# Rows of the feed-forward blocks transposed by DMAs instead of by TensorE, in a cross attention and mixture-of-experts kernel

## The reference

```python
def attention(Q, K, V, causal):
    scores = einsum('bqd,bkd->bqk', Q, K) / sqrt(d_k)          # causal: masked
    return einsum('bqk,bkd->bqd', softmax(scores), V)
def xattn(y, Z):                                               # no projections
    y = layernorm(y + attention(y, y, y, causal=True), g1, beta1)
    y = layernorm(y + attention(y, Z, Z, causal=False), g2, beta2)
    ff = relu(y @ w1 + b1) @ w2 + b2                           # 256 -> 1024 -> 256
    return layernorm(y + ff, g3, beta3)
def moe(h):                                                    # 8 experts, each row uses 2
    topk_w, topk_idx = top_k(softmax(h @ wg.T), 2)             # weights normed to 1
    return sum over the two of weight * ((silu(h @ w1[e].T) * (h @ w3[e].T)) @ w2[e].T)
x = x + xattn(layernorm(x), ctx)
x = x + moe(layernorm(x))
```

## Time and profile before

| | us |
|---|---|
| median of 3 runs | 558.45 (558.25 to 559.0) |
| the profiled execution, own time | 560.24 |
| its span, first to last instruction | 557.8 |
| TensorE busy in the span | 503.5 (90%) |
| VectorE, ScalarE, GpSimd busy | 383.5, 291.2, 294.7 |
| mean granted clock of TensorE | 0.982 of full |

### The profile page before, as it was taken

One profiled execution on the slowest core, in us unless ns is written; L12 is line 12 of the kernel. 1 busy time (PEld: TensorE's weight loads), 2 busy tenths in 40 slices (PEclk: granted clock), 3 DMA queues, 4 the chain that ended last, 5 costly groups with the idle time before them and its releaser, 6 DMA issues. The chain is left out here.

```text
span 557.8 us, 11154 instructions
## 1 busy us (share of the span) xinstructions
PE 503.5 (90%) x3753; PEld 333.2 (60%) x3753; DVE 383.5 (69%) x977; ACT 291.2 (52%) x592; POOL 294.7 (53%) x331
## 2 busy tenths in 40 slices
PE   4999999979899998899999977779999899999981
PEld 2676766745566675577565666545566556666651
DVE  5799886688877577867876789988767534344440
ACT  2647867574747546673558373564554333443420
POOL 3564030016423519826795629473667565667564
PEclk9999999999999999999999999999999999999995
DMA  8021615238878257832765543125795688787763
GB/s 273 2 71 25 198 58 152 77 71 160 155 170 141 86 73 145 175 90 77 147 142 135 162 101 125 39 76 105 122 182 97 114 113 124 131 127 132 132 86 38
DMA packets 131090, 64.57 MB, mean 116 GB/s; under 512 B 105533, under 2 KB 122366, under 8 KB 131038
## 3 DMA queue, kind: packets, MB, share of 16 engines
q1 hardware_dynamic: 123550, 53.64, 44.2%
q0 software_dynamic: 7488, 10.23, 11.5%
HBM read 28.19 MB, written 10.35 MB: 69 GB/s over the span
## 5 line engine op out<-in xcount | busy, mean ns | idle before, releaser
L1132 PE MATMUL ps<-arena,probT 128*128 128x256 f16 (+2 forms) x1092 | 181.8, 320 | 7.0 <-DMA probT<-prob 4.4
L1132 PEld LDWEIGHTS ps<-arena,probT 128*128 128x128 f16 (+1 forms) x1092 | 105.8, 98 | 65.5 <-issue 10.3
L901 POOL DMA_INDIRECT out<-y,qst x39 | 62.5, 1604 | 28.3 <-issue 13.9
L946 ACT ACTIVATE prob<-ps,nbias 128x512 f16<-128x512 f32 x64 | 39.0, 610 | 71.5 <-DVE nbias L1647 71.5
L1132 PE MATMUL ps<-arena,qT 128*128 128x512 f16 (+1 forms) x384 | 70.8, 337 | 5.4 <-DVE prob L1782 5.3
L2181 DVE SCALAR_TENSOR_TENSOR ps<-ps,w1m 128x512 f32<-128x512 f32 x39 | 27.4, 703 | 54.6 <-ACT w1m L1075 54.5
L1075 ACT ACTIVATE w1m<-ps 128x512 f32<-128x512 f32 x39 | 23.3, 597 | 75.5 <-PE ps L1132 75.5
L1132 PE MATMUL ps<-arena,tT 128*128 x468 | 58.2, 276 | 2.8 <-DVE tT L2277 2.8
L1132 PEld LDWEIGHTS ps<-arena,qT 128*128 128x128 f16 x384 | 33.0, 98 | 41.2 <-issue 8.4
L1132 PE MATMUL ps<-tT 128*128 128x512 f16 (+3 forms) x240 | 52.7, 360 | 2.1 <-DVE tT L1609 2.1
L1132 PE MATMUL ps<-w2s,tT 128*128 128x256 f16 x384 | 48.4, 273 | 5.7 <-DVE tT L1850 5.6
(11 more groups left out here) (216 smaller groups left out, 983.0 us busy)
## 6 DMA issues: line engine op xcount, KB each, us to landing
stage<-we_in SPq DMA_DIRECT2D x33, 256.0 KB, 2.9
prob<-we_in SPq DMA_DIRECT2D x15, 256.0 KB, 2.9
xin<-x_in SPq DMA_DIRECT2D x16, 128.0 KB, 2.8
out<-y SPq DMA_DIRECT2D x16, 128.0 KB
hrow<-tT SPq DMA_DIRECT2D x4, 512.0 KB, 3.1
y<-x_in SPq DMA_DIRECT2D x3, 512.0 KB, 6.4
stage<-z_in SPq DMA_DIRECT2D x4, 256.0 KB, 5.2
prob<-w_in SPq DMA_DIRECT2D x4, 256.0 KB, 2.9
```

Of the source, the lines that this page charges most:

```text
L901: g.indirect_dma_start(out[:rows_of(p), :], bass.IndirectOffsetOnAxis(ridx[:, n:n + 1], 0), ys[:, n % RING, :], None, compute_op=ALU.add). ...
L946: a.activation(row_cols(q, 0, c), ps[c][:, :w], ACT.Exp, bias=nbias[:, q, :], scale=SM)
L1132: r = t.matmul(o, lhs(a), rhs(b), start=first and n == 0, stop=last and n == 2)
```

## The change

For tiles 0 to 13 the rows of `y` no longer go through TensorE. Tile by tile, ScalarE copies the row tile to 16 bits (`y_row_hi`), VectorE subtracts (`y_row_lo`), and SP issues two DMA transposes of 128x256 (`y_turn`). The halves lie in `nrm`, the buffer of the layer norm on GpSimd, for tiles 0 to 11 (so `ln_affine` waits for the transposes two tiles back), and in the query row's place for tiles 12 and 13. Only unit 4 keeps the transposes on TensorE. Three orders change too: SP issues a step's three transposes of exponentials ahead of the step's weight loads, not one ahead and two behind; VectorE's norm of the last self-attention block stands behind the low halves of step 1, not ahead of them; in the last expert tile VectorE's copy of the transposed rows stands ahead of the scaling of the tile before. In units 1 and 2 ScalarE's copy of `h` moves behind the first relu. Left out below: new semaphores, a shorter `psY`, and calls of `y_trans` and `y_lo` that go or lose an argument.

```diff
--- before.py
+++ after.py
@@ -209,6 +209,19 @@
             return stage[:, t % 2, CH:PW].bitcast(F16)[:, :2 * D]
+        def y_row(n):
+            return nrm[:, n % 2, :].bitcast(F16) if n < 3 * TB else q_row(n)
+        def y_turned(n, a):
+            m = n % TB
+            if n < 3 * TB:
+                home = prow if a else ph.rearrange("p (q c) -> p q c", q=2)
+                return home[:, :, ROW + m * P:ROW + (m + 1) * P]
+            at = a * 2 * NT * P + ROW
+            return ph[:, at:at + KD * 2 * P].rearrange("p (k c) -> p k c", k=KD)[:, :, m * P:(m + 1) * P]
@@ -606,6 +619,17 @@
+            def y_turn(n):
+                wait(sp, "y_rlo", n + 1)
+                if n >= TB:
+                    wait(sp, "f_up", KF * (n // TB))
+                else:
+                    wait(sp, "s_pv", NT)
+                for a in range(2):
+                    sp.dma_start_transpose(y_turned(n, a), y_row(n)[:, a * D:(a + 1) * D]
+                                           ).then_inc(sm[f"y_t{n % 2}"], 16)
             def loads(n0, n1):
@@ -616,12 +640,13 @@
             for i in range(NT - 1):
+                if i - 1 in FIRST and i < NT - 2:
+                    y_turn(i - 2)
                 if i + 3 < NT:
                     q_turn(i + 3)
-                turn(i + 1, 0)
+                for p in range(len(TURNS)):
+                    turn(i + 1, p)
                 loads(step_from(i), step_from(i) + STEP_PIECES[i])
-                turn(i + 1, 1)
-                turn(i + 1, 2)
                 if i == 0:
@@ -632,6 +657,8 @@
                     if u == 2:
+                        y_turn(NT - 4)
+                        y_turn(NT - 3)
                         for m in range(6):
@@ -639,6 +666,8 @@
                     load_x(n)
+                if 0 < i < NT - 3 and i not in FIRST:
+                    y_turn(i - 1)
@@ -735,6 +764,8 @@
                 pool.wait_ge(sm[pre + "rstd"], i + 1)
+                if 2 <= i < 3 * TB + 2:
+                    pool.wait_ge(sm[f"y_t{q}"], 32 * (i // 2))
                 g.tensor_scalar(nrm[:, q, :], u[:, q, :], mv[:, q, 0:1], rstd[:, q, :], ALU.subtract,
@@ -780,7 +811,9 @@
-                wait(pool, "f_ytr", j + 1 if j < 3 else len(UNITS))
+                wait(pool, "y_rlo", min(TB * (j + 1), NT - 2))
+                if j == NB - 1:
+                    wait(pool, "f_ytr", 1)
                 for m in range(TB):
@@ -988,16 +1021,22 @@
                     c_exps(i + 1, c)
-                    if i == NT - 2 and c == 0:
-                        y_hi(3)
                 if i + 4 < NT:
                     q_hi(i + 4)
                 split_step(split_hi, act_, i + 1)
-            def y_hi(u):
-                wait(act_, "f_ytr", u + 1)
+                if 0 < i < NT - 2:
+                    y_row_hi(i - 1)
+            def y_row_hi(n):
+                wait(act_, "c_y", n + 1)
+                if n >= 3 * TB:
+                    wait(act_, f"c_q{n % 2}", 16 * ((n - 1) // 2 + 1))
+                copy(y_row(n)[:, :D], y[:, n, :]).then_inc(sm["y_rhi"], 1)
+            def y_hi():
+                wait(act_, "f_ytr", 1)
                 for k in range(KD):
-                    copy(ybT(u, 0, k)[:, cols(u)], psY(u, k)).then_inc(sm["f_yhi"], 1)
+                    copy(ybT(4, 0, k)[:, cols(4)], psY(k)).then_inc(sm["f_yhi"], 1)
@@ -1032,6 +1071,12 @@
                     relu(u, f)
+                    if u in (1, 2) and f == 0:
+                        h_hi(u - 1)
+                    if u < 3 and f == 4:
+                        y_row_hi(TB * (u + 1))
+                    if u == 2 and f == 5:
+                        y_row_hi(NT - 3)
                     if u in (1, 2) and f in (3, 4):
@@ -1050,18 +1095,14 @@
                 else:
-                    c_exps(i + 1, 0)
-                    y_hi(u)
-                    for c in range(1, C_CH):
+                    for c in range(C_CH):
                         c_exps(i + 1, c)
                     if i + 4 < NT:
                         q_hi(i + 4)
-                    if u:
-                        h_hi(u - 1)
                 ffn(u)
                 if not last:
                     split_step(split_hi, act_, i + 1)
-            y_hi(4)
+            y_hi()
             ffn(4)
@@ -1259,25 +1300,23 @@
-            def y_trans(u, i):
-                j, m0, n = UNITS[u]
-                pe.wait_ge(sm["c_y"], TB * j + m0 + n)
-                if u == 0:
-                    pe.wait_ge(sm["c_qlo"], 3)
-                elif u < 4:
-                    wait(pe, "n_u", TB * u)
-                else:
-                    pe.wait_ge(sm["c_u"], NT)
+            def y_trans():
+                j, m0, n = UNITS[4]
+                wait(pe, "c_y", NT)
+                wait(pe, "c_u", NT)
                 for k in range(KD):
                     for m in range(n):
-                        r = t.transpose(psY(u, k)[:, m * P:(m + 1) * P], y[:, TB * j + m0 + m, k * P:(k + 1) * P],
+                        r = t.transpose(psY(k)[:, m * P:(m + 1) * P], y[:, TB * j + m0 + m, k * P:(k + 1) * P],
                                         ident[:])
                 r.then_inc(sm["f_ytr"], 1)
             def up(u, f):
                 n, w = u * KF + f, UNITS[u][2] * P
-                if f == 0:
-                    wait(pe, "f_ylo", KD * (u + 1))
+                if f == 0 and u < 4:
+                    for q in range(2):
+                        wait(pe, f"y_t{q}", 32 * ((UNITS[u][0] * TB + UNITS[u][2]) // 2))
+                elif f == 0:
+                    wait(pe, "f_ylo", KD)
                 if u < 4 and f < 3:
@@ -1294,7 +1333,8 @@
                 if f == 0:
-                    wait(pe, "f_ylo", KD * (u + 1))
+                    if u == 4:
+                        wait(pe, "f_ylo", KD)
                     if u != 3:
@@ -1806,8 +1843,6 @@
                 q = i % 2
-                if i == 0:
-                    s_norm(NB - 1)
                 split_step(split_lo, dve, i)
@@ -1823,9 +1858,9 @@
                 early[0]()
-                if i == NT - 2:
-                    y_lo(3)
                 between(early[1:], own)
+                if i == 0:
+                    s_norm(NB - 1)
                 sums("c_", 1 - q, C_CH, i + 1, C_CH * (i + 2))
@@ -1833,15 +1868,21 @@
                     x1_aggr(FIRST[i - 3])
+                if 0 < i < NT - 2:
+                    y_row_lo(i - 1)
                 for f in late:
                     f()
                 if late:
                     c_bias(i + 2, q)
-            def y_lo(un):
+            def y_row_lo(n):
+                wait(dve, "y_rhi", n + 1)
+                v.tensor_tensor(y_row(n)[:, D:], y[:, n, :], y_row(n)[:, :D], ALU.subtract).then_inc(sm["y_rlo"], 1)
+            def y_lo():
                 for k in range(KD):
-                    wait(dve, "f_yhi", KD * un + k + 1)
-                    v.tensor_tensor(ybT(un, 1, k)[:, cols(un)], psY(un, k), ybT(un, 0, k)[:, cols(un)],
+                    wait(dve, "f_yhi", k + 1)
+                    v.tensor_tensor(ybT(4, 1, k)[:, cols(4)], psY(k), ybT(4, 0, k)[:, cols(4)],
                                     ALU.subtract).then_inc(sm["f_ylo"], 1)
@@ -2081,9 +2122,7 @@
                 split_step(split_lo, dve, i)
-                c_los(i + 1, 0)
-                y_lo(un)
-                for c in range(1, C_CH):
+                for c in range(C_CH):
                     c_los(i + 1, c)
@@ -2100,6 +2139,10 @@
                     split_chunk(split_lo, dve, un, f)
+                    if f == 5:
+                        y_row_lo(TB * (un + 1))
+                    if un == 2 and f == 6:
+                        y_row_lo(NT - 3)
                     if un and f == 5:
@@ -2272,10 +2315,10 @@
             e_step(NJ - 1, (NJ - 1) % RING, NJ - 3)
-            weighted(NJ - 2, (NJ - 2) % RING)
             wait(dve, "e_ltr", 2)
             v.tensor_copy(actT[:, (NJ - 1) % RING, 1].rearrange("p k c -> p (k c)"),
                           last_bank(1)).then_inc(sm["e_lcp"], 1)
+            weighted(NJ - 2, (NJ - 2) % RING)
             weighted(NJ - 1, (NJ - 1) % RING)
```

More of the change, by code:

```diff
@@ L291, in xattn_ffn_moe @@
             c_rstd c_nrm c_gam c_y c_qtr c_qhi c_qlo c_q0 c_q1
-            f_ytr f_yhi f_ylo f_up f_hi f_lo f_dn f_down f_xb
+            y_rhi y_rlo y_t0 y_t1 f_ytr f_yhi f_ylo f_up f_hi f_lo f_dn f_down f_xb
             n_yb n_u n_stat n_agg n_var n_rstd n_nrm n_gam n_cen n_x1 x2_in0 x2_in1
@@ L497, in xattn_ffn_moe, with psY @@
         ACT_END = 14
-        def psY(u, k):
-            return (psO[k] if u == 4 else psT[k])[:, :UNITS[u][2] * P]
+        def psY(k):
+            return psO[k][:, :UNITS[4][2] * P]
         def q_cols(t):
@@ L1366, in _ @@
                 if i not in AFTER:
-                    if i == NT - 2:
-                        y_trans(3, NT - 1)
                     c_step(i)
@@ L1371, in _ @@
                 u = AFTER[i]
-                y_trans(u, i)
                 c_pv(i)
@@ L1466, in _ @@
```

(4 more changed lines are left out.)

## The result

| | before | after |
|---|---|---|
| median of 4 runs each, us | 558.5 (558.3 to 559.0) | 579.2 (577.6 to 580.7) |
| profiled execution, its span, us | 560.2, 557.8 | 580.3, 578.5 |
| mean granted clock | 0.982 | 0.975 |

The account below looks back on a forecast made before the run. It took VectorE's loop, as long as TensorE's work beside it, to bound cross attention. Terms +16.8 to the first down-projection, -1.8 and -0.5 gave +14.5: profiled 574.7, median 573.0 us, range 563 to 580.

Parts of the forecast that it names:

- main case: Whole kernel: slower, 573.0 us, own range 565 to 578; chance 0.67.
- C: Rival, steps 1 and 4: rows' high half made early enough, so half the loss, about 564 us; chance 0.08.
- E: Rival, steps 7, 8, 11, 12: SP's queue needs 9.8 us in a step of 8.8, about 577 us; chance 0.10.
- main term: Steps 1 to 4: VectorE's maxima wait for late loads through split and row; four intervals 54.7 us against 37.8, +16.9.
- The split of that sum: Four intervals' 16.9 us: 11.6 from loads behind all three transposes, the rest from the row's place behind the split.
- I take no loss from SP's own time: SP's two transposes per row, 2.7 us, fit because the steps have grown; no loss.
- Rival D: Steps 1 to 4: TensorE, idle 4 to 5 us each, stays at 1.2 GHz and becomes the bound; 584 us; chance 0.06.
- Step 0: Moved norm ends TensorE's 2.57 us idle, but nbias of tile 2 hardly moves: +0.3 us; -2.0 without the VectorE-GpSimd clash.
- Start of the first block: First up-projection at 188.95 instead of 173.76, +15.2, with 2 us less at its start; lower clock behind it costs 1.57.
- Blocks 2 and 3: Feed-forward blocks: 0.9 us saved each, -1.8; at worst 0, at best 1.5 each; steps 6-8, 10-12 get 0.4 each.
- unit 3: At 322.87: four TensorE transposes go, -0.5 us.
- sign of an error: Prediction wrong if first up-projection starts before 180 us, or steps 7 to 12 grow by more than 1 us each.

Follow-up runs that it names:

- e1: Changed kernel with ScalarE making the high half of the row of y ahead of the weight split, not behind it; 565.1 us, ratio 1.013.
- e3: Changed kernel with the row of y ahead of ScalarE's split and SP's weight loads back between first and second transpose; 564.7 us, ratio 1.009.
- e12: e3 with each high row's transpose cut in two of half size, same bytes, one more SP issue per row; 575.2 us, ratio 1.029.
- e6: Kernel before with weight loads ahead of a step's first transpose and the last self-attention norm behind the row of q; 556.2 us, ratio 0.996.

## Why the prediction was right, and where it was off

**The number: inside the range, near its end.** I forecast 573.0 us and measured 579.2. That is above the 578 at which the main case's own range ended, and within 563 to 580 only by the room that I had added for rivals C and E. Of +14.5 us I had the main term's mechanism and most of its size; that the whole stayed in the range owes something to luck.

**Main mechanism: right.** The chain load, split, row, low half, maxima was where I put it, with my numbers in step 1: 13.27 us measured against 13.35.

**Size of the four intervals: +19.5, not +16.9.** The mis-sized term is the landing of a load that follows three transposes. I took 3.0 us; in step 1 it was 3.0 (137.23 to 140.24), in step 2 4.3 (150.57 to 154.84), above the 3.9 that I had as the most. These two loads also took SP 2.15 us to issue, against 1.06. From 112 to 200 us weight loads landed after 3.0 to 4.2 us, 3.7 in the median; before, after 2.5 to 3.8, 3.0 in the median. Steps 2 to 4 came to 15.3, 14.5 and 14.2 against 14.0, 14.0 and 13.35.

**The split of that sum into 11.6 for the loads and 5.3 for the rows: half wrong.** Undoing the loads took 12.5 us off the intervals, near enough, but undoing the rows' place took 14.5, not 5.3. A step goes by the longest of its chains, not by their sum, and e1 to e3 show three others close beneath: ScalarE's late split alone (43 us for four steps), SP's issue time (10.6 us a step in e3) and VectorE's old loop (8.8).

**"I take no loss from SP's own time": right for steps 1 to 4 of this kernel, for the reason given,** that the steps had grown. It hid a cost which shows once they shrink: e3 is still 0.9% slower. My rival E had that mechanism but placed it in steps 7, 8, 11 and 12, where a third issue per row changes nothing (e12). What SP costs in e3 is paid in the steps ahead of the first block.

**Rival D did not come.** TensorE was idle 4.7 and 4.9 us before the scores of tiles 4 and 5, which then took 6.18 and 7.04 us, and it still waited 3.15 us for VectorE ahead of the next, which took 4.24: VectorE's chain stayed the longer one. The 5.65 us in D's favour stand in no row; rows 2 have 5.81 us after 2.57 of idle.

**Step 0: right.** I said +0.3, it was -0.2 (12.24 us from one `nbias` to the next against 12.42). VectorE's row of q took 2.53 us at 125.84 beside GpSimd's first multiplication, instead of 1.90 beside the second and 0.41 alone (e6). The Trainium skill's rule that the prediction cites (SBUF — State Buffer, Who interferes with whom) agrees with these times.

**Start of the first block: right.** From `nbias` of tile 6 to the first up-projection 2.42 us instead of 4.29, 1.9 less (I said 2.0). The lower clock behind it cost 2.1 us, not 1.6: the sum over values of tile 6 stands 18.6 us later (217.25 against 198.68), the up-projection 16.5.

**Blocks 2 and 3: 0, not -1.8, and unit 3: 0, not -0.5.** Here I was too kind to the rows. The intervals that hold blocks 2 and 3 did shrink, by 2.0 and 1.3 us, but the six steps took 3.9 us where I had charged 0.4 each, 2.4. Units 1 and 2 begin with 1.60 us of waiting for the last transposed row (the row at 252.24 above), which SP issues at 249.00, behind three transposes, two stores and a load. And steps 7 and 11 grew by 1.3 us, over the 1 us that I had named as the sign of an error; the other four grew by 0.3. VectorE's two halves meet GpSimd's operations there:

```profile
235.03 0.83 DVE L1727 TENSOR_TENSOR stage<-y,stage 128x256 f16<-128x256 f32 x1
235.78 0.94 DVE L1880 TENSOR_TENSOR nrm<-y,nrm 128x256 f16<-128x256 f32 x1
```

```profile
234.86 3.14 POOL L859 TENSOR_TENSOR y<-y,vec 128x256 f32<-128x256 f32 x4
```

where the row of q took 0.41 in the same step before. In unit 3 TensorE's 1.35 us of idle became

```profile
341.99 3.24 PE L1173 MATMUL ps<-arena,probT 128*128 128x256 f16 x28 [1.89 <-issue]
```

**Behind unit 4: +2.1, which I had at 0.** 1.4 of it is the second gather of the experts, for which TensorE waits 3.22 us instead of 1.85:

```profile
387.35 0.40 PE L1448 MATMUL ps<-ident,y 128*128 128x128 f16 x4 [3.22 <-DMA y<-hrow,qst]
```

In the kernels that transpose the rows of `y` by DMA this wait is 2.4 to 3.6 us, in those that do not 1.4 to 2.0. Why is not shown.

In all: the stretch up to 112 us happened to be 1.0 us shorter, then -0.2, +19.5, -1.9, +2.1, 0, 0, +2.1, which is the 20.7 us between the spans; I had 14.5. But for the first two, the misses lie on one side, and most of them are waits for a queue or an engine that I took to be free.

## What to carry to other kernels

Before a transpose is moved from TensorE to DMAs, add up the issue time on the issuing queue per step, not the bytes: here a transpose costs SP about 1.2 us at either of two sizes, so a block's eight take 9.7 us of SP, and the eight of TensorE that they replace took 1.07 us together. Count what prepares the rows as well: VectorE's low halves, two of them beside GpSimd's work, lengthened six steps by 3.9 us. When two edits lengthen one step, ask for the longest chain with each of them alone; undoing either may give back nearly all. And look on in-order engines for what stands behind a wait: a load issued late costs ScalarE idle time, and a row queued behind it costs everyone.

## What the runs showed of the hardware

A DMA transpose from SBUF to SBUF mostly took SP 1.17 to 1.26 us to issue for 128x256 and 1.20 us for half of that, and landed in 2.3 to 3.1 us in the median of a run; a plain load of weights took 0.33 to 0.6 us to issue where SP's queue was not crowded, and two behind three transposes up to 2.2. Three transposes of the exponentials in a row took 4.1 to 4.8 us of SP, and in the crowded queues of e3 and e12 the last of them alone took up to 2.75 and 3.15. A VectorE subtraction of two SBUF operands took 2.53 us beside a GpSimd multiplication of 2.35 us, 0.8 to 0.9 beside short ones, 0.41 alone. And the end of the program varied from 209.8 to 216.8 us between profiles, with granted clocks of 0.83 to 0.93 in the last 40 us: positions in the trace told apart what medians of ten runs could not.
